# Experts' weights split into two parts by VectorE in attention's last iteration, in memory beneath finished buffers

## What is computed

```
x = x + layernorm(attention(layernorm(x)))     # 16 heads of 8; elu(q)+1, elu(k)+1, rope; softmax;
                                               # plus a 3-tap convolution of v along the rows (lepe)
x = x + layernorm(ffn(layernorm(x)))
# ffn: 8 experts, the 2 best per row by a softmax gate, plus one shared expert for all rows
h1 = xt @ w1[e].T + b1[e];  h3 = xt @ w3[e].T + b3[e]
g, l = (h1*h3)[even], (h1*h3)[odd];  a = min(g,7) * sigmoid(1.702*min(g,7)) * (clip(l,-7,7) + 1)
y[e] = a @ w2[e].T + b2[e];  routed = sum of the two experts' y, weighted;  out = routed + shared
```

## Time and profile before

| | |
|---|---|
| median of three runs | 1266.2 us |
| profiled execution: own time, span | 1265.12 us, 1263.3 us |
| mean granted TensorE clock | 0.943 of full |
| busy: PE, DVE, ACT, POOL | 1059.5, 1071.7, 937.9, 833.7 us |
| end of attention's last copy (ACT line 885) | 883.92 us |
| first instructions of the experts' stage | 884.5 us |
| WALL on ACT, WALL on DVE | 18 instructions each, 884.5 to 902.9 us |

### The profile page before, as it was taken

How to read it: one execution, slowest core, us unless ns; L and a number is a source line. 1 busy time by engine, 2 the same in 40 slices (tenths; PEclk the granted TensorE clock), 3 DMA queues, 4 the chain that set the end, 5 groups by cost and what they waited for, 6 DMA issues and landing times. The chain is left out here.

```text
span 1263.3 us, 21973 instructions
## 1 busy us (share of the span) xinstructions
PE 1059.5 (84%) x6376; PEld 445.4 (35%) x6376; DVE 1071.7 (85%) x2451; ACT 937.9 (74%) x1782; POOL 833.7 (66%) x1087
## 2 busy tenths in 40 slices
PE   1498989999999999999998999898799999887810
PEld 0012222222322222222222222222578778655600
DVE  2398899999999999999999999991687889999944
ACT  1117888888888878788788788889699898867712
POOL 5445466676578787888778878645364546776475
PEclk9559999999999999999999999999799999999965
DMA  2453332422423334234233242203134544454412
GB/s 67 116 133 122 97 87 65 107 83 74 115 69 111 90 99 115 79 102 120 68 103 104 78 110 84 73 19 111 51 100 137 192 157 156 129 152 132 120 51 80
DMA packets 108982, 128.20 MB, mean 101 GB/s; under 512 B 14224, under 2 KB 81844, under 8 KB 108596
## 3 DMA queue, kind: packets, MB, share of 16 engines
q1 hardware_dynamic: 98848, 105.94, 29.5%
q0 software_dynamic: 8192, 16.79, 4.7%
q10 hardware_dynamic: 1824, 4.06, 0.9%
HBM read 58.85 MB, written 59.51 MB: 94 GB/s over the span
## 5 line engine op out<-in xcount | busy, mean ns | idle before, releaser
L1075 DVE TENSOR_REDUCE MX<-psS 128x1 f32<-128x512 f32 x1024 | 647.0, 679 | 64.8 <-PE psS L762 63.0
L974 ACT ACTIVATE PR<-psST 128x512 f32<-128x512 f32 x986 | 535.9, 600 | 127.3 <-PE psST L750 125.2
L762 PE MATMUL psS<-KS,QS 48*128 48x512 bf16 x1024 | 371.3, 400 | 40.8 <-DMA KS<-scratch_parts 23.8
L750 PE MATMUL psST<-QS,KS 51*128 51x512 bf16 x986 | 337.6, 385 | 42.3 <-ACT PR L974 25.8
L776 PE MATMUL psPV<-PR,V 128*32 128x512 f32 x2048 | 274.3, 608 | 5.8 <-ACT PR L974 1.0
L750 PEld LDWEIGHTS psST<-QS,KS 51*128 51x128 bf16 x986 | 78.5, 93 | 398.9 <-ACT PR L974 370.0
L1968 POOL DMA_INDIRECT SHARED<-scratch_y,FROM x128 | 130.2, 1017 | 51.6 <-issue 37.9
L465 POOL DMA_INDIRECT scratch_x<-XN,POSI x128 | 128.6, 1005 | 36.3 <-issue 34.0
L762 PEld LDWEIGHTS psS<-KS,QS 48*128 48x128 bf16 x1024 | 87.8, 93 | 105.5 <-DVE MX L1075 73.5
L1533 PE MATMUL psY<-WD,HA 128*128 (+1 forms) x496 | 67.7, 279 | 13.3 <-issue 6.9
L1507 PE MATMUL psH<-XH,WS 128*128 128x512 f32 x169 | 74.0, 438 | 2.9 <-DVE XL L1720 2.0
(11 more groups left out here) (217 smaller groups left out, 1845.7 us busy)
## 6 DMA issues: line engine op xcount, KB each, us to landing
scratch_parts<-PT SPq DMA_DIRECT2D x192, 128.0 KB, 2.4
QS<-scratch_parts SPq DMA_DIRECT2D x64, 192.0 KB, 3.3
KS<-scratch_parts SPq DMA_DIRECT2D x64, 192.0 KB, 4.2
XR<-scratch_x SPq DMA_DIRECT2D x46, 256.0 KB, 2.8
scratch_y<-YR SPq DMA_DIRECT2D x46, 256.0 KB, 2.0
RES<-EL SPq DMA_DIRECT2D x64, 128.0 KB, 2.0
scratch_x<-ZERO SPq DMA_DIRECT2D x18, 256.0 KB
X<-in_x SPq DMA_DIRECT2D x16, 256.0 KB, 4.7
```

The source lines that it names most:

```text
L750: nc.tensor.matmul(bank(st_banks(t), k)[:], KS[t.par][rows, h // 2, kc * P:(kc + 1) * P], QS[t.par][rows, h // 2, :], start=True, stop=Tru ...
L762: nc.tensor.matmul(bank(psS, k)[:], QS[b.par][rows, h // 2, qc * P:(qc + 1) * P], KS[b.par][rows, h // 2, :], start=True, stop=True).then_ ...
L974: nc.scalar.activation(PR[:, s % 2, HEAD_AT[j], :], bank(st_banks(t), k)[:], ACT.Exp, scale=SCALE).then_inc(st_exp, 1)
L1075: nc.vector.tensor_reduce(out=MX[:, qc, h:h + 1], in_=bank(psS, k)[:], axis=AX.X, op=ALU.max).then_inc(s_max, 1)
```

## The change

WALL is allocated in the outermost scope, first of all, at an address `arena`. Attention's COS, SIN, XT, EXQ, EL, RES, QS0 and KS0 are no allocations of their own any more: they lie at fixed offsets inside WALL's 36,864 bytes, which they fill exactly. Both parts of the weights are made by DVE in iteration 15, in tile place j = 2 of slots 1 to 10: first a wait for all that still reads or writes the buffers beneath (`wall_free`), then in each slot the high parts of one expert (a DVE copy, two instructions) and the low parts of the expert before it (two subtractions). ACT's and DVE's work on WALL in the experts' stage is gone, and the waits on `split` there ask for all nine.

```
+        def beneath_wall(at, name, shape, dt):
+            return nc.alloc_sbuf_tensor_at(name, shape, dt, offset=arena + at)
-        COS = sb("COS", [P, N], F32)
+        ROW_BYTES = 4 * N
+        COS = beneath_wall(0, "COS", [P, N], F32)
...
-        QS = [sb(f"QS{i}", [P, PAIRS, N], BF16) for i in range(2)]
+        QS = [beneath_wall(10 * ROW_BYTES, "QS0", [P, PAIRS, N], BF16), sb("QS1", [P, PAIRS, N], BF16)]
...
+            SPLIT_ORDER = (NE, *range(NE))
+            def wall_free():
+                dve.wait_ge(st_psum, (B - 1) * TILES)
+                dve.wait_ge(vT_psum, B)
+                for w in range(2):
+                    dve.wait_ge(turned[w], 32 * B)
+                    dve.wait_ge(rot_cos[w], B)
+                    dve.wait_ge(rot_sin[w], B)
+                    dve.wait_ge(part2[w], B)
+                    dve.wait_ge(part3[w], B)
+                dve.wait_ge(weights, 16 * WEIGHTS)
+            def weights_high(n):
+                e = SPLIT_ORDER[n]
+                for m, W in enumerate((W1, W3)):
+                    last = nc.vector.tensor_copy(WALL[:, e, 0, m], W[:, e].rearrange("p (f g) -> p g f", g=2))
+                last.then_inc(high, 1)
+            def weights_low(n):
+                e = SPLIT_ORDER[n]
+                dve.wait_ge(high, n + 1)
+                for m, W in enumerate((W1, W3)):
+                    last = nc.vector.tensor_tensor(WALL[:, e, 1, m], W[:, e].rearrange("p (f g) -> p g f", g=2),
+                                                   WALL[:, e, 0, m].bitcast(F32), ALU.subtract)
+                last.then_inc(split, 1)
...
                 for s in range(SLOTS):
                     for j in range(HG):
+                        if t.c == B - 1 and j == 2 and 1 <= s <= EXP_ALL + 1:
+                            if s == 1:
+                                wall_free()
+                            if s <= EXP_ALL:
+                                weights_high(s - 1)
+                            if s > 1:
+                                weights_low(s - 2)
...
                     elif p == 0:
-                        pe.wait_ge(split, 1)
+                        pe.wait_ge(split, EXP_ALL)
...
-            def weights_high(e):
-                for m, W in enumerate((W1, W3)):
-                    last = nc.scalar.activation(WALL[:, e, 0, m], W[:, e].rearrange("p (f g) -> p g f", g=2), ACT.Copy)
-                last.then_inc(high, 1)
...
-            weights_high(NE)
             turn(0)
...
-                if p + 1 < len(SPLIT_AT):
-                    for e in range(SPLIT_AT[p], SPLIT_AT[p + 1]):
-                        weights_high(e)
...
-            weights_low(0, NE)
             turn(0)
...
-                if p + 1 < len(SPLIT_AT):
-                    for e in range(SPLIT_AT[p], SPLIT_AT[p + 1]):
-                        weights_low(e + 1, e)
                 drain(p)
...
+        arena = -(-nc.sbuf_base // 32) * 32
+        WALL = sb("WALL", [P, EXP_ALL, 2, 2, 2, F], F32R)
+        split = ctx.enter_context(nc.semaphore("weights_split"))
```

More of the change, by code:

```diff
@@ L469, in attention @@
 def attention(nc, ends, x_in, wqkvT, chan, ones, rope_cos, rope_sin, ident, numbers, count, gate_wT, gate_b,
-              X, WD, IDF, TAB, ZERO, BD, XN2, CW, BASE, XG, scattered, zero_filled, weights, halved, table, load_weights):
+              X, WD, IDF, TAB, ZERO, BD, XN2, CW, BASE, XG, scattered, zero_filled, weights, halved, table, load_weights,
+              W1, W3, WALL, arena, split):
     nc.disable_value_cache = True
@@ L485, in attention @@
         BP1 = sb("BP1", [P, 2], F32)
-        COS = sb("COS", [P, N], F32)
-        SIN = sb("SIN", [P, N], F32)
+        ROW_BYTES = 4 * N
+        COS = beneath_wall(0, "COS", [P, N], F32)
+        SIN = beneath_wall(ROW_BYTES, "SIN", [P, N], F32)
         ST0 = sb("ST0", [P, QC, 6], F32)
@@ L496, in attention @@
         MR = sb("MR", [P, 2, QC, HALF], F32)
-        XT = sb("XT", [P, 2, N], F32)
-        EXQ = sb("EXQ", [P, 2, N], F32)
+        XT = beneath_wall(2 * ROW_BYTES, "XT", [P, 2, N], F32)
+        EXQ = beneath_wall(4 * ROW_BYTES, "EXQ", [P, 2, N], F32)
         ROT = ends.ROT
-        EL = sb("EL", [P, 2, N], F32)
-        RES = sb("RES", [P, 2, N], F32)
+        EL = beneath_wall(6 * ROW_BYTES, "EL", [P, 2, N], F32)
+        RES = beneath_wall(8 * ROW_BYTES, "RES", [P, 2, N], F32)
         PT = sb("PT", [P, 2, PARTS, N], BF16)
@@ L506, in attention @@
         MT = sb("MT", [PARTS * HALF, 2, N], BF16)
-        QS = [sb(f"QS{i}", [P, PAIRS, N], BF16) for i in range(2)]
-        KS = [sb(f"KS{i}", [P, PAIRS, N], BF16) for i in range(2)]
+        QS = [beneath_wall(10 * ROW_BYTES, "QS0", [P, PAIRS, N], BF16), sb("QS1", [P, PAIRS, N], BF16)]
+        KS = [beneath_wall(14 * ROW_BYTES, "KS0", [P, PAIRS, N], BF16), sb("KS1", [P, PAIRS, N], BF16)]
         V = [sb(f"V{i}", [P, QC, H, VW], F32) for i in range(2)]
@@ L522, in attention @@
         SCM = nc.dram_tensor("scratch_max", [2, 2, PARTS * HALF, N], BF16, kind="Internal").ap()
+        high = sem("weights_high")
         consts = sem("consts_loaded")
@@ L1244, in unit_tables, with experts @@
         nc.vector.tensor_scalar(ROW[:, units], UNIT[:, 0:UNITS[st]], float(ROOM * NE), None, ALU.min).then_inc(row_ready, 1)
-def experts(nc, ends, W1, W3, WD, BD, halved, X, IDF, TAB, ZERO, XN2, POS, WSEL, CW, CNT, XG, XTD, scattered,
+def experts(nc, ends, W1, W3, WALL, split, WD, BD, halved, X, IDF, TAB, ZERO, XN2, POS, WSEL, CW, CNT, XG, XTD, scattered,
             zero_filled, table, BASE, DROP, EXPERT, ROW, expert_ready, row_ready, out):
@@ L1264, in experts @@
         GATHERS = QC * TOPK
-        SPLIT_AT = (0, 4, 8)
         RANKED = 19
@@ L1300, in pool_clips @@
             return p <= LAST[0]
-        WALL = sb("WALL", [P, EXP_ALL, 2, 2, 2, F], F32R)
         WS = sb("WS", [P, W_BUFS, 2, 2, 2, F], F32R)
@@ L1347, in experts @@
         count_ready, from_step = sem("count_ready"), sem("from_step")
-        high, split = sem("weights_high"), sem("weights_split")
         cw_psum, cwT_ready = sem("cw_psum"), sem("cwT_ready")
@@ L1629, in evict @@
                     if i < R_EARLY:
-                        act.wait_ge(split, min(2 * (i // 2) + 3, EXP_ALL))
+                        act.wait_ge(split, EXP_ALL)
                     elif i < R_BUFS:
@@ L1704, in _ @@
         def _(dve):
[L1705 to L1710, removed]
             def turn(p):
@@ L2050, in build @@
         attention(nc, ends, x, wqkvT, chan, ones, cos, sin, ident, table, count, gate_wT, gate_b,
-                  X, WD, IDF, TAB, ZERO, BD, XN2, CW, BASE, XG, scattered, zero_filled, weights, halved, unit_table, load_weights)
-        experts(nc, ends, W1, W3, WD, BD, halved, X, IDF, TAB, ZERO, XN2, POS, WSEL, CW, CNT, XG, XTD, scattered,
+                  X, WD, IDF, TAB, ZERO, BD, XN2, CW, BASE, XG, scattered, zero_filled, weights, halved, unit_table, load_weights,
+                  W1, W3, WALL, arena, split)
+        experts(nc, ends, W1, W3, WALL, split, WD, BD, halved, X, IDF, TAB, ZERO, XN2, POS, WSEL, CW, CNT, XG, XTD, scattered,
                 zero_filled, unit_table, BASE, DROP, EXPERT, ROW, expert_ready, row_ready, out)
```

## The result

| | before | after |
|---|---|---|
| median, 20 runs each | 1266.55 us | 1263.62 us |
| lowest to highest | 1264.7 to 1269.25 | 1261.2 to 1264.68 |
| profiled execution: own time, span | 1265.12, 1263.3 us | 1263.11, 1261.2 us |

The ratio is 0.9975 [0.9969, 0.9982]: 2.9 us, or 0.25%, faster. The forecast was 6.1 us faster, 1260.1. The direction was right and the time lies inside the range; the size was less than half.

A forecast was written before the change was run, and what follows sets the result against it. At the handover PE idled 7.98 us for `y_ready`, bound by DVE's program order, fed by ACT's. A 5.3 us earlier sum plus 0.8 us of clock gave 6.1 us: 1260.1 from 1266.2, range 1257.8 to 1264 (8 in 10).

The forecast's parts named there:

- The cover on DVE: Attention's iteration 15: DVE's idle 6.24 and 6.09 us hide its new copies and subtractions; path cost 0, slack 4.8 us.
- The cover on POOL: End of attention: POOL pays some 7 us for sharing ports with DVE, absorbed by idle time inside and 7.53 us at its end.
- The shift: Handover to the experts: without the splitting there, L271 starts about 897.5 instead of 902.82, saving 5.3 us.
- The clock term: PE's restart after the handover: less idle time means less low clock, saving 0.8 us, bounds 0 and 2.5.
- The shift is kept to the end: From the routed units to the last gathers: PE and POOL carry the whole 6.1 us gain to the kernel's end.
- rival B: After the handover: the gain is lost in a later wait; 1266.2 us, or 1264.2; chance 0.08 together with D.
- D: Attention's iteration 15: waits ahead of the writes hold until late, so no gain, 1266 us; chance 0.08 together with B.
- A: Handover: PE's clock doesn't fall at all, saving 7.8 us, 1258.4 us; chance 0.13.
- C: Attention's iteration 15: POOL holds up DVE through shared ports, making PE wait 11 us; 1271 us; chance 0.07.

The follow-up runs named there:

- The fillers: Groups of matmuls whose results nobody reads, added on PE; in the changed kernel 0.995 with one at `y_ready`, 0.995 with one at the handover.
- the reorder: Kernel before with one line moved: in place 1 DVE does `drain` ahead of the subtractions for experts 4 to 7; 1263.59 us, 0.9984 (earlier chip 0.9894).
- the filler at `y_ready`: Changed kernel plus ten unused matmuls on PE ahead of its wait for `y_ready`; 1258.73 us, 0.995 of before.
- the repeat: Changed kernel again, unedited, on the chip where before took 1265.53 us; 1261.8 us, 0.9974.
- both fillers: Changed kernel plus ten unused matmuls ahead of the `y_ready` wait and thirteen around attention's end; 1257.97 us, 0.9936 of before.
- before with the filler: Kernel before plus 32 unused matmuls on PE ahead of its wait for `y_ready`; 1263.56 us, 0.9986 of before.
- doubled work: Changed kernel with each of DVE's new copies and subtractions done a second time in the same slot; 1269.43 us, 1.0036 of before.
- the first repeat of the change: Changed kernel again, unedited, on the chip where before took 1336.51 us; ratio 0.9949.

## Why the prediction was right and wrong

**The cover on DVE held.** The work cost nothing on DVE's or PE's path: L271 of batch 14 comes 17.82 us after line 294 in both kernels (865.86 - 848.04 and 867.76 - 849.94). The rows of 856.93 and 857.33 hold two copies in 0.48 us and two subtractions in 0.75, 0.24 and 0.37 each, where I took 0.35 for either. The Trainium skill (VectorE: DVE Perf Modes, "The perf-mode tier table") puts an fp32 copy at twice the rate of a `tensor_tensor`; the medians, 282 and 411 ns, go that way.

**The cover on POOL was read wrongly, and held by luck.** I wrote that POOL has idle time inside and 7.53 us at its end. The idle time inside that counted was 3.41 us ahead of line 402, and it is all gone: POOL's last scatter ended 868.23 - 848.04 = 20.19 us after line 294 before, and 873.52 - 849.94 = 23.58 after, 3.39 later, and line 402 follows it at once. The 7.53 us are no slack but a fixed part of the path to the barrier. So the start of the stage moved by 0.07 us (36.45 to 36.52 after line 294); one more us of contention would have moved it by one. That POOL pays was right, in half the size (3.4 us, I had some 7). DVE paid too: two copies took 1.46 us beside POOL where 0.48 was usual; the longest took 1361 ns, 1.08 over the median, about one of POOL's operations there (0.83 to 1.32 us). The Trainium skill (SBUF — State Buffer, "SBUF: two separate sides") speaks of an exclusive lock that whoever starts first holds; this trace agrees in so far as either engine is held up by about the other's instruction, and it corrects my reading that only POOL waits.

**The shift was right.** L271 starts 18.33 - 13.07 = 5.26 us earlier relative to the stage, where I had 5.3; PE's idle time is 2.66 us, where I had 2.7; and the steps on the way came as worked out (first A, gate, HA, L, L271, 2.55 us from A to A).

**The clock term is the step that failed.** I took +0.8 us, "If the clock falls anyway at 898.3, as in this profile, and returns 3.5 after", with 0 as the lower bound, and allowed for no loss. It was -0.95: logits to WS went from 8.57 to 9.52. The clock did fall at the restart, as supposed, but it stayed low for 6.8 us and not 3.5. The two stretches that I took for the size, 3.5 and 5.2 us, were only what was left of longer ones when PE restarted: the first ran from 881.2 to 888.0, the second from 898.3 to 908.5. Of the second, 5.3 us passed while PE stood still and cost nothing, and the other 5.0 were paid. After, PE was idle from 897.60, the clock fell at 900.3, at the restart, and the 6.8 us that followed were paid whole. The shorter wait took away the free part of the stretch and left the paid part. I treated the cost as something that shrinks with the wait and bounded it from one side only.

The fillers show that the low clock is what was lost: without it after the restart the same 5.26 us shift reaches the first routed unit with 23.04 - 20.12 = 2.9 us more, and the time falls by 0.24%, 3.0 us. By the forecast no more than 2.5 - 0.8 = 1.7 us of low clock would have been left there.

The exact -0.95 is in part a draw. The changed kernel without fillers took 9.52, 9.41, 7.92 and 6.28 us from logits to WS in its four profiles, after 2.65 or 2.66 us of idle time in each (low for 6.8, 6.7, 3.4 and 0 us after the restart). After 7.98 and 7.96 us of idle time it was 8.57 and 9.19, after 5.11 and 5.10 (the reorder, in its two profiles) 9.93 and 8.88. So the length of the idle time alone doesn't tell the cost. Whether the changed kernel pays more than the one before on average isn't settled: the filler at `y_ready` brought 3.0 us to it and 2.0 to the one before, each known to a microsecond or two only.

**What I took as given: 5.3 + 0.8 = 6.1. What came: 5.26 - 0.95 = 4.31 us at the first WS product,** 4.59 in the repeat. Of this 2.9 us are in the medians of the first comparison and 3.7 in the repeat's (3.3 by its ratio). So 0.9 to 1.4 us do not arrive, which is the smaller second error ("The shift is kept to the end"): I gave rival B 0.08 together with D. The profiled pair's spans differ by 2.1 us: 4.31, less the 1.97 by which the stage starts later (1.90 of it stand ahead of the change's first instruction), less 0.24 behind the first WS product, from where to the end of the span before took 351.18 us and the change 351.42. In the repeat that last part took 352.5 us, with both fillers 353.5, so more is lost there. One wait in it grows. PE waits longer for the routed units' rows when it comes to them earlier, here line 1485 of before and line 1529 of the kernel with both fillers, 900 to 1245 (total, times, longest):

```profile
PE psX L1485 <- DMA XR<-scratch_x: 1.1, 3, 0.5
```

```profile
PE psX L1529 <- DMA XR<-scratch_x: 2.4, 5, 0.9
```

It is 1.6 us in the change and 1.7 in its repeat, which could be 0.5 to 0.6 us of the gap; but it is 1.9 in before with the filler and with the reorder too, so this is not shown. Where the rest goes stays open.

**The rivals.** A (the clock doesn't fall, 7.8 us saved, 1258.4) is what the filler at `y_ready` made: 1258.73 from 1264.81, 6.1 us saved, though 27.63 - 20.12 = 7.5 had come at WS. It needed work for PE, or luck, not a shorter wait. B holds for a fifth to a third of what the handover gained. C needed 10.9 us of delay; the real limit was 3.4 us on POOL, so it was nearer than I had it, and at doubled work a loss over before is what happens (1269.43). D is out: the copies start from 850.7 on. Two slips stand in the text of the forecast: its range begins at "A's 1257.8", where A's sum is 1258.4, and the granted clock has a low slice in the middle of the experts' stage too (a 7 in the earlier trace rows), in both kernels.

**A version that beats both.** The changed kernel with both fillers runs at 0.9936 [0.9923, 0.9949] of before, 7.6 us faster by the medians and 8.1 by the ratio, and 3.8 us under the change.

## What to carry to other kernels

Shortening a wait of TensorE isn't worth exactly its length, where its clock falls while it waits. Read from the windows where the granted clock falls and rises against where the engine is idle, and count only the part of the low stretch in which it works: a wait cut to a third can cost more clock than the long one did. One trace gives one draw of this, so take it from several, or compare a kernel in which the engine is kept busy through the wait. Before calling an engine's last idle time slack, compare it over several traces: one that has the same length everywhere is a part of the path.

## What the runs showed of the hardware that I had not expected

- The low clock after the same idle time of 2.65 us differed from trace to trace: 6.8, 6.7, 3.4 and 0 us in four profiles of one kernel.
- POOL's end to the next stage's start is 7.53 us in every trace where POOL is last, whether its chain ended early or 8.8 us late.
- With a low clock at attention's end (in the change a mean of 0.61 from 883, then 0.50) ACT's last copy waits 2.14 us, at the high clock 1.27 or 1.20; this 0.87 us doesn't move the stage's start where POOL sets it (884.49 and 886.46 above).
- DVE's copies and POOL's operations stretch each other: a copy of 282 ns took up to 1361, four normalisations on POOL 4.43 us against 3.12, a scatter's issue 1.75 against 0.96. Over the iteration POOL lost 3.4 us to 36 DVE instructions.
- On the three chips with 70 to 90 us more the traces have waits such as this one of the first repeat of the change, its releaser no engine of this core (total, times, longest); the traces of the other chips don't:

```profile
DVE L L1756 <- remote: 46.9, 5, 15.8
```
